# A two-layer vision tower on one core: new orders on the engines from the second attention's softmax to the second router's scatters

## The reference, cut to what matters

```
qkv  = layernorm(h) @ w_qkv + b_qkv
dots = th1 . (q k^T / 8)                       (8 heads mixed into 8)
attn = th2 . softmax(dots)
h    = h + (attn v) @ w_out + b_out
x    = layernorm(h)
p    = softmax(x @ Wg); the two best experts of each token
slot = expert * C + rank of the token among those of its expert
buf[slot] = x  (tokens past the capacity C are dropped)
h    = h + weighted sum of the two experts' outputs
```

## Time and profile before

| what | us |
|---|---|
| plain runs, median of 3 | 210.89 |
| plain runs, lowest and highest | 209.28, 211.78 |
| profiled execution, span from first to last instruction | 214.1 |
| PE busy in it | 179.6 |
| DVE, ACT, POOL busy in it | 101.6, 73.2, 79.4 |

### The profile page before, as it was taken

How to read it: one execution, slowest core, us unless ns; L and a number is a source line. 1 busy time by engine, 2 the same in 40 slices (tenths; PEclk the granted TensorE clock), 3 DMA queues, 4 the chain that set the end, 5 groups by cost and what they waited for, 6 DMA issues and landing times.

```text
span 214.1 us, 3836 instructions
## 1 busy us (share of the span) xinstructions
PE 179.6 (84%) x1347; PEld 135.6 (63%) x1351; DVE 101.6 (47%) x373; ACT 73.2 (34%) x219; POOL 79.4 (37%) x104
## 2 busy tenths in 40 slices
PE   6979799989899899999999889968787969986400
PEld 2946467777687699999687565457664436655200
DVE  0037676978453127882217618363446713333104
ACT  2002253543425445665510554083214002332100
POOL 8008341500875037886502300001156602565510
PEclk9995999996558999999999999979999985998855
DMA  6959999980121429981140179940011153111142
GB/s 183 291 156 307 367 294 346 368 350 5 36 52 26 101 57 318 301 327 40 37 119 4 48 225 428 318 112 0 3 33 37 38 118 48 42 34 35 32 124 53
DMA packets 18956, 31.12 MB, mean 145 GB/s; under 512 B 4838, under 2 KB 12517, under 8 KB 18554
## 3 DMA queue, kind: packets, MB, share of 16 engines
q1 hardware_dynamic: 15552, 27.15, 39.5%
q0 software_dynamic: 2784, 3.31, 6.0%
q10 hardware_dynamic: 602, 0.42, 0.7%
HBM read 23.52 MB, written 7.40 MB: 144 GB/s over the span
## 4 chain that ended last, share of the span: by engine, by line
PE 53%; POOL 12%; DMA 12%; issue 11%; DVE 5%; ACT 2%; SPq 2%; POOLq 1%; ACTq 0%; DVEq 0%
PE ps L1330 50%; POOL rooms L587 5%; DMA patchesT<-in_patchesT 4%; POOL rooms L549 4%; DMA xb<-rooms 2%; POOL o_rows L595 2%; DVE xn L866 2%; POOL ln_rstd L525 2%; PE ps L1788 1%; DMA o_tok<-o_rows 1%; DMA rooms<-xm,slot 1%; DMA rooms<-xm,room 1%; DMA o_rows<-o_sb,result_row 1%; SPq L411 1%; PE ps L1575 1%
## 5 line engine op out<-in xcount | busy, mean ns | idle before, releaser
L556 POOL DMA_INDIRECT o_rows<-o_sb,result_row x16 | 21.0, 1312 | 18.1 <-DVE o_sb L1073 15.7
L525 POOL TENSOR_TENSOR ln_rstd<-ln_var,minus_half 119x1 f32<-119x1 f32 x12 | 6.7, 566 | 51.3 <-DVE ln_var L860 51.3
L728 ACT ACTIVATE hid_b<-ps,w_ring 128x128 f32<-128x128 f32 x64 | 18.3, 369 | 14.2 <-PE ps L1330 13.4
L595 POOL DMA_INDIRECT o_rows<-o_sb,result_row x16 | 15.1, 943 | 18.7 <-DVE o_sb L1301 15.6
L549 POOL DMA_INDIRECT rooms<-xm,room x10 | 11.4, 1144 | 15.8 <-issue 15.8
L1330 PE MATMUL ps<-w_ring,hid_b 128*128 128x128 f32 x128 | 17.0, 276 | 0.3 <-ACT hid_b L728 0.3
L1330 PE MATMUL ps<-xbT,w_ring 128*128 128x128 f32 x128 | 17.0, 275 | 0.0
L1330 PE MATMUL ps<-filler 128*128 128x512 bf16 x51 | 15.4, 433 | 1.7 <-DVE filler L878 1.5
L824 ACT ACTIVATE hid<-ps,moe_b 128x64 f32<-128x64 f32 x32 | 8.3, 311 | 24.0 <-PE ps L1330 18.6
L1330 PEld LDWEIGHTS ps<-w_ring,hid_b 128*128 128x128 f32 x128 | 15.6, 192 | 0.5 <-ACT hid_b L728 0.5
L1330 PEld LDWEIGHTS ps<-xbT,w_ring 128*128 128x128 f32 x128 | 15.6, 192 | 0.0
(11 more groups left out here) (209 smaller groups left out, 361.8 us busy)
## 6 DMA issues: line engine op xcount, KB each, us to landing
w_ring<-in_w_routed SPq DMA_DIRECT2D x16, 514.0 KB
m<-in_m SPq DMA_DIRECT2D x2, 2048.0 KB, 13.0
rooms<-zeros SPq DMA_DIRECT2D x8, 330.0 KB, 5.4
patchesT<-in_patchesT SPq DMA_DIRECT2D x6, 272.0 KB, 5.3
xb<-rooms SPq DMA_DIRECT2D x16, 66.0 KB
w_s<-in_w_s SPq DMA_DIRECT2D x2, 512.0 KB, 5.9
moe_b<-in_moe_b SPq DMA_DIRECT2D x2, 512.0 KB, 16.9
rooms<-zeros SPq DMA_DIRECT2D x1, 792.0 KB, 6.7
```

The source lines that it names most:

```text
L525: nc.gpsimd.tensor_tensor(ln_rstd[:, g:g + 1], ln_var[:, g:g + 1], minus_half[:], ALU.pow).then_inc(rstd_ready, 1)
L556: nc.gpsimd.indirect_dma_start(o_rows[:], bass.IndirectOffsetOnAxis(ap=result_row[:, b:b + 1], axis=0), o_sb[:, b, :], None).then_inc(o_sc ...
L595: nc.gpsimd.indirect_dma_start(o_rows[:], bass.IndirectOffsetOnAxis(ap=result_row2[0:past_, j:j + 1], axis=0), o2_sb[0:past_, j, :], None) ...
L728: nc.scalar.activation(hid_b[:, b % RING, c, :], ps[:, b % 2, c * BS:(c + 1) * BS], ACT.Gelu, bias=w_ring[:, b % WRING, FF + c:FF + c + 1] ...
```

## The change

It does the following. The scores of the batches 2 and 3 go to the banks 0 and 1 in place of 4 and 5, and `dots(b)` for b of 2 and more waits until the bank's earlier scores were read. ACT does all four `exponents` ahead of the first `held_to`, and its Sqrt ahead of `folded_out(1)`. PE does `held(0)` ahead of `folded(1)` and no longer waits for all scores to be read before it; that wait now stands before `project(0)`. PE does `router_turn(0)` ahead of `held(3)`, and one `fill` goes. DVE does `normalised3(g)` and `place2(g-1)` ahead of `attended(g+1)`. ACT does `router_out(0)` and `second_copy(0)` ahead of the last two `held_to`, and each `router_out` ahead of a `deviation3`.

```
--- before.py
+++ after.py
@@ -47,7 +47,7 @@
 BATCH = 2
 BATCHES = GRPS // BATCH
 A_BANKS = (2, 3, 6, 7)
-DOTS_BANK = (0, 1, 4, 5)
+DOTS_BANK = (0, 1, 0, 1)
 OUT_BANK = 0
 EM = 32
 CAP = int(np.ceil(1.25 * 2 * T / EM))
@@ -778,13 +778,13 @@
             keys_to(1, 7)
             exponents(1)
             folded_out(0)
+            exponents(2)
+            exponents(3)
             held_to(0)
             held_to(1)
-            exponents(2)
-            exponents(3)
+            nc.scalar.activation(warm[:], eps_col[0:1, 0:1], ACT.Sqrt)
             folded_out(1)
-            nc.scalar.activation(warm[:], eps_col[0:1, 0:1], ACT.Sqrt)
-            for grp in range(2, GRPS):
+            for grp in range(2, 6):
                 held_to(grp)
 
             def deviation3(g):
@@ -798,15 +798,17 @@
                 nc.scalar.copy(xT[:, cols(g)], ps[:, ROUTER_BANK[g], 0:rows(g)]).then_inc(xT_ready, 1)
 
             router_out(0)
+            second_copy(0, 3)
+            held_to(6)
+            held_to(7)
+            router_out(1)
             deviation3(2)
-            second_copy(0, 3)
-            router_out(1)
             second_copy(1, 3)
+            router_out(2)
             deviation3(3)
-            router_out(2)
             second_copy(2, 3)
+            router_out(3)
             deviation3(4)
-            router_out(3)
             second_copy(3, 3)
             router_out(4)
             second_copy(4, 3)
@@ -1232,28 +1234,28 @@
             attended(0)
             aggregate(3, 0)
             variance(3, 0)
+            normalised3(0)
             attended(1)
-            normalised3(0)
             aggregate(3, 1)
             variance(3, 1)
             pick2(0)
             mark2(0)
+            normalised3(1)
+            place2(0)
             attended(2)
-            normalised3(1)
             aggregate(3, 2)
-            place2(0)
             pick2(1)
             mark2(1)
+            normalised3(2)
+            place2(1)
             attended(3)
-            normalised3(2)
             aggregate(3, 3)
-            place2(1)
             pick2(2)
             mark2(2)
+            normalised3(3)
+            place2(2)
             attended(4)
-            normalised3(3)
             aggregate(3, 4)
-            place2(2)
             pick2(3)
             mark2(3)
             normalised3(4)
@@ -1654,6 +1656,8 @@
 
             def dots(b):
 
+                if b >= 2:
+                    pe.wait_ge(dots_read, b - 1)
                 for s_ in range(BATCH):
                     for i in range(PER):
                         at = S * (PER * (BATCH * b + s_) + i)
@@ -1739,18 +1743,17 @@
             pe.wait_ge(keys_out, 2 * H)
             dots(2)
             dots(3)
+            pe.wait_ge(xq_loaded, 16 * PER)
+            held(0)
             folded(1)
-            pe.wait_ge(xq_loaded, 16 * PER)
+            held(1)
+            pe.wait_ge(wf_out, 2)
             pe.wait_ge(dots_read, BATCHES)
-            held(0)
-            pe.wait_ge(wf_out, 2)
-            held(1)
             project(0)
             held(2)
             project(1)
+            router_turn(0)
             held(3)
-            router_turn(0)
-            fill(1, 3)
             router_logits(0)
             project(2)
             slot_ranks(0)
```

## The result

The changed kernel takes 202.43 us (median of 4 runs, 201.11 to 203.65) against 210.35 us before (median of 4, 209.28 to 211.78): a ratio of 0.9635 with a 95% interval of 0.956 to 0.9709. Forecast were 204.3 us and 202.0 to 208.0. Medians are of all runs, while a ratio leaves out runs that were more than 1.5% above the fastest of their kernel, so the two can differ.

What follows compares the result with a forecast made beforehand. Bound: a chain of waits through ACT, PE and POOL's ten scatters, so `project(0)`'s start and the groups' pace count. 2.7 + 1.16 + 1.7 + 1.1 - 0.1 = 6.6 us off gave 204.3 us; range 202.0 to 208.0.

Steps and rivals of the forecast that it cites:

- Softmax and folding: Up to `project(0)`: with PE's new order it starts at about 139.7, not 142.43, 2.7 us gained.
- The clock at `project(0)`: `project(0)` on PE: without the still stand it takes 2.0 us, not 3.17; 1.16 gained, bounds 0 and 1.16.
- Rival A: At `project(0)` and `held(1)`: plain runs may not all drop to 1.2 GHz; gain 5.0, so 205.9 us; chance 0.15.
- From `project(1)` to the first scatter: Router start, 6.1 us before: turn 0.95, logits 0.24, `place2(0)` 0.5 earlier; together 1.7 us gained.
- The pace: Router groups up to the third pair of scatters: 3.4 to 3.5 us a group, not 4.05; 1.1 us gained.
- The ring: Router, PE's own cycle per group: `project` 2.0, `slot_ranks` about 0.5, turn to next `project` 0.9; 3.4 to 3.5 us.
- The fourth slot: POOL's scatters after the third pair: this slot comes some 0.2 us later than POOL could take it.
- What follows the scatters: Constants and experts behind the tenth scatter: unchanged, counted at nothing; the constants' matmuls move along within 0.4 us.
- rival C: First three expert pairs run at the higher clock: 2.0 us more, 8.6 in all, 202.3 us; chance 0.08.
- E: Late part: four more stops of 1.40 us, as before POOL's scatter at 188.06, leave 1.0 gained, 209.9 us; chance 0.09.
- B: Router: ranks come late, the ring does not shorten and the 1.7 goes too; 3.9 remain, 207.0 us; chance 0.12.
- D: Experts: the clock stays at 1.2 GHz, 13 other pairs cost 0.66 us each, 212.9 us; chance 0.06.

Runs made afterwards that it cites:

- the second profiles: The kernel before and the changed kernel, both without edit, profiled and timed once more: 202.77 us against 210.37, ratio 0.9681.
- act_sqrt: The changed kernel with exponents 2 and 3 behind `held_to(0)` and `held_to(1)` as before, Sqrt still ahead of `folded_out(1)`: 202.02 us, a single run.
- fill_gap: The kernel before with ten matmuls on constants in TensorE's 2.4 us of standing still, no order changed: ratio to before 1.0005.
- fill_gap2: The kernel before with ten matmuls on constants in TensorE's 2.4 us of standing still, run again in a second set: ratio to before 0.9853.
- dve_old: The changed kernel with only VectorE's router order put back as before: 206.02 us against 202.77, ratio to before 0.9862.
- fills_28: The changed kernel with 28 in place of 32 matmuls on constants between router and experts: 203.09 us, ratio to before 0.9598.

## Why the prediction was right

Its mechanism held in the stretch of the change, its sum of 6.6 us was 1.3 short of the measured 7.9, and the range held the time. Some of that is luck: the stretch gave 7.3 to 7.4, the late part 1.3 to 1.5 that the forecast had put at nothing, and in these profiles a later start of the scores took 0.5 to 0.9 back. The span itself was missed by 6.0 us (207.5 forecast, 201.5 measured), mostly for the 4.6 us of stops in the first profile of before; taking the difference off the median kept them out of the forecast time.

- *Softmax and folding*, 2.7 forecast: `project(0)` starts 2.85 us earlier against the scores, 2.38 between the second profiles. TensorE has no hole, and the table load lay in ScalarE's hole as forecast. The forecast named the exponents as what was late and TensorE's order as the way out; act_sqrt shows that the second alone does it. It also saw the table load as the one dangerous edit, but looked at the wrong side: the place ahead of `folded_out(1)` is not a risk of 1.5 us but a gain of 0.7, for behind it the load would have held up `held_to(2)`.
- *The clock at `project(0)`*, 1.16 forecast, 1.16 between the first profiles and 1.61 between the second; with the step above, 4.0 in both pairs. fill_gap and fill_gap2 show the cause alone. Rival A (the clock's share is the profile's own) is not refuted for plain runs. As the Trainium skill has it ("TensorE: Matmul & The Clock Gate", section "What's actually happening"), the number of slow matmuls varies from run to run; here which ones were slow did vary (`held(1)` in one profile of before, `held(2)` in the other), but every profile with the hole had a slow `project(0)` and none without.
- *From `project(1)` to the first scatter*, 1.7 forecast, 1.98 measured. The turn did not wait, and the logits came 0.9 us after it, not 1.0.
- *The pace*, 1.1 forecast, 1.44 measured: the mis-sized term. The ring was named rightly as TensorE's (dve_old shows that VectorE's order was the old one), though ScalarE's copy stands in it. From the end of one `project` to the start of the next it takes 1.2 us, then 1.3 (148.01 to 149.23, 151.21 to 152.54), not the 1.4 to 1.5 that the sum of ranks and turn gave: the turn begins 0.2 to 0.3 after `project` ends, not 0.5, since the ranks' matmuls overlap with `project` and with the turn at their ends, and from turn to `project` it takes 1.0, not 0.9.
- *The fourth slot*, said to come 0.2 too late for POOL, came in time (6.96 us from the third pair to the tenth scatter, as before).
- *What follows the scatters*, counted at nothing: 1.3 to 1.5 us were there, rival C in part. By the forecast's own sign this part was wrong: it was not to change by over a microsecond, and it fell by 6.05 us between the first profiles and by 1.3 between the second. In both profiles of the changed kernel the chain even goes through the constants, so the late part did not hang on the tenth scatter's landing there. The step that failed is that the constants move along "within 0.4" and so change nothing; in all fourteen profiles the first experts were slow where TensorE stood still for 1.4 us or more between the constants and the first rows, and fast where it didn't. Rival C's 2.0 was near in size. E's stops belonged to one execution.

Rivals B (the ring does not shorten) and D (slower) did not happen: the ring is 3.3 us, and no profile had more than four slow pairs at the start of the experts.

## What to carry to other kernels

When an engine waits for a result at the end of a long chain, look for independent work that stands ahead of the chain in some engine's queue: here a weight product of 3.7 us stood in front of 0.75 us of matmuls, and with the two exchanged the hole of 2.4 us is gone even with ScalarE's exponents in their old place (act_sqrt). In a ring over several engines, finish the next turn's input while the long instruction of this turn runs; the order of one in-order engine was worth 3.0 us in five groups. Put a table load into a hole of its engine, and after any reordering look at the whole stretch behind it for the clock.

## What the runs showed that I had not expected

TensorE's clock fell in the changed kernel while the engine was never idle for long: 0.79 granted in 155.9 to 158.7 with 2.43 of 2.80 us busy, then 0.50 for 5.3 us with the engine busy in all of them. A constant took 0.43 us there and 0.21 later. The constants ended at 169.27 where the first rows were used by VectorE at 168.15, so they held the experts' start up by about 1 us. That cost little in the end: in fills_28 the first transpose came 0.8 us sooner after the tenth scatter (5.45 against 6.27), and the late part was only 0.2 to 0.35 us shorter. And a profile of one execution can hold some 4.6 us of stops (44.71 against 40.14 behind the scatters) that the next execution of the same kernel doesn't have: the difference of two spans, 12.6 us here, is not the change's worth.
